# Interleaving the K and V weight transposes with their matmuls, splitting the Wd load, and sharing the softmax masks between VectorE and GpSimd

## What is computed

```python
xn = layernorm(x)
Q, K, V = heads(xn @ Wq.T + bq), heads(xn @ Wk.T + bk), heads(xn @ Wv.T + bv)   # 16 heads of 64
mask = (col <= row & row - col <= 128) | (row < 1) | (col < 1)
attn = softmax(where(mask, Q @ K.T / 8, -1e9)) @ V
a    = attn @ Wo.T + bo
w    = top-1 routing of xn @ W_router over 2 experts
r    = sum_e w[e] * ((silu(xn @ Wg[e]) * (xn @ Wu[e])) @ Wd[e])
s    = (silu(xn @ Sg) * (xn @ Su)) @ Sd
out  = x + a + r + s
```

## Time and profile before

| | |
|---|---|
| two runs | 1678.94 and 1824.74 us, median 1751.84 |
| the profiled execution | 1677.85 us |
| its span, slowest core (core 3) | 1676.1 us |
| spans of the eight cores | 1663.5 to 1676.1 us |
| PE busy / DVE / ACT / POOL, share of the span | 89% / 33% / 18% / 12% |
| mean granted TensorE clock, core 3 | 0.893 |

### The profile page before, as it was taken

The page is one execution under the profiler, slowest core; times in us unless marked ns, Lnnn a source line. Parts: engine busy times, 40 slices in busy tenths (PEclk is TensorE's granted clock), DMA queues, the critical chain, the costliest instruction groups (busy, mean ns, idle before and its releaser), DMA issues.

```text
span 1676.1 us, 26894 instructions; the slowest of 8 cores (1663.5 to 1676.1 us)
## 1 busy us (share of the span) xinstructions
PE 1487.0 (89%) x8424; PEld 721.0 (43%) x8424; DVE 555.7 (33%) x1187; ACT 301.1 (18%) x579; POOL 196.1 (12%) x258
## 2 busy tenths in 40 slices
PE   3566889769899878999999999999999999999893
PEld 2233434336666333444444444444444444444341
DVE  2432223367777421006641100066411000333332
ACT  2322220125555102330000023300000232000000
POOL 1000000000000121111111111111122111110211
PEclk9977898855555799999999999999999999999996
DMA  6220311200001253576531224764455437742776
GB/s 120 74 76 13 51 24 28 39 7 21 21 21 40 54 104 51 51 89 73 54 45 75 78 55 41 90 86 43 47 77 77 53 38 95 89 41 62 144 152 135
DMA packets 150812, 106.28 MB, mean 63 GB/s; under 512 B 105746, under 2 KB 126354, under 8 KB 150674
## 3 DMA queue, kind: packets, MB, share of 16 engines
q0 software_dynamic: 133664, 75.72, 33.9%
q1 hardware_dynamic: 7794, 16.27, 3.2%
q10 hardware_dynamic: 9216, 12.59, 3.2%
HBM read 117.60 MB, written 33.29 MB: 90 GB/s over the span
## 4 chain that ended last, share of the span: by engine, by line
PE 77%; DMA 12%; DVE 4%; issue 3%; ACT 3%; POOL 0%; DVEq 0%; POOLq 0%; SPq 0%; ACTq 0%
PE pb L827 20%; PE pb L809 20%; PE pb L881 14%; PE pb L347 7%; DMA out<-sto 6%; PE pb L640 4%; PE pb L381 3%; PE pb L600 3%; PE pb L649 2%; DMA pscr<-sto 2%; PE pb L760 1%; DMA ovl<-Wq 1%; ACT exT L618 1%; PE pbT L327 1%; DVE sto L897 1%
## 5 line engine op out<-in xcount | busy, mean ns | idle before, releaser
L881 PE MATMUL pb<-big 128*128 128x512 bf16 x1536 | 334.8, 381 | 7.3 <-DVE sto L897 7.2
L809 PE MATMUL pb<-xnT,stg 128*128 128x512 bf16 x1536 | 332.2, 379 | 0.4 <-ACT big L813 0.4
L827 PE MATMUL pb<-xnT,stg 128*128 128x512 bf16 x1536 | 332.0, 379 | 0.0
L831 DVE TENSOR_TENSOR big<-big,pb 128x512 bf16<-128x512 bf16 x192 | 132.0, 687 | 462.0 <-PE pb L827 461.9
L881 PEld LDWEIGHTS pb<-big 128*128 128x128 bf16 x1536 | 150.5, 98 | 191.1 <-issue 11.9
L813 ACT ACTIVATE big<-pb 128x512 bf16<-128x512 f32 x192 | 114.6, 597 | 657.1 <-PE pb L809 656.9
L809 PEld LDWEIGHTS pb<-xnT,stg 128*128 128x128 bf16 x1536 | 150.2, 98 | 181.8 <-issue 0.9
L827 PEld LDWEIGHTS pb<-xnT,stg 128*128 128x128 bf16 x1536 | 150.3, 98 | 181.2 <-issue 0.2
L618 ACT ACTIVATE exT<-pb 128x385 bf16<-128x385 f32 (+2 forms) x256 | 107.3, 473 | 107.9 <-PE pb L600 55.3
L347 PE MATMUL pb<-xnT,ovl 128*128 128x512 bf16 x512 | 120.3, 400 | 0.0
L902 DVE COPY sto<-pb 128x512 f32<-128x512 f32 x64 | 41.9, 687 | 178.9 <-PE pb L881 178.2
(11 more groups left out here) (136 smaller groups left out, 784.0 us busy)
## 6 DMA issues: line engine op xcount, KB each, us to landing
out<-sto POOLq DMA_DIRECT2D x96, 256.0 KB, 4.4
stg<-Wg POOLq DMA_DIRECT2D x32, 256.0 KB, 4.4
stg<-Wu POOLq DMA_DIRECT2D x32, 256.0 KB, 4.4
big<-Wd POOLq DMA_DIRECT2D x4, 2048.0 KB, 16.3
stxr<-x ACTq DMA_DIRECT2D x32, 256.0 KB, 4.7
stx<-x SPq DMA_DIRECT2D x8, 512.0 KB, 3.9
sto<-x SPq DMA_DIRECT2D x8, 512.0 KB, 3.7
pscr<-sto POOLq DMA_DIRECT2D x32, 128.0 KB, 2.6
```

Of the source, the lines that this page charges most:

```text
L809: add("tensor", (lambda f_=f_, ncs=ncs, td=td, bank=bank, sg=sg: (lambda t: t.matmul(pb[bank][:, 0:512], sg[:, 128 * td:128 * (td + 1)], x ...
L827: add("tensor", (lambda f_=f_, ncs=ncs, td=td, bank=bank, sg=sg: (lambda t: t.matmul(pb[bank][:, 0:512], sg[:, 128 * td:128 * (td + 1)], x ...
L831: add("vector", (lambda f_=f_, ncs=ncs, bank=bank: (lambda v: v.tensor_mul(big[:, H_OFF + T * f_ + 512 * ncs:H_OFF + T * f_ + 512 * (ncs + ...
L881: add("tensor", (lambda f_=f_, ntile=ntile, bk=bkv, woff=woff: (lambda t: t.matmul(pb[bk][:, 0:512], big[:, H_OFF + T * f_ + 128 * ntile:H ...
```

## The change

It has four parts. (1) The transposes of the four Wk quarters are no longer done in one piece: after each quarter come the 8 K groups that read it, by `gen_kt_itpair`. The loads move along. (2) V runs half by half: after the quarters 0 and 1 of Wv all 16 groups with ih = 0, after the quarter 3 all with ih = 1, with the quarters 2 and 3 of Wv, and then the quarters 0 and 1 of Wo, placed between runs of 8 groups. The bias DMA is started earlier. `vgen_one` itself is as before. (3) The masks of odd heads are multiplied on POOL. (4) Each down-weight buffer is loaded by four DMAs of a quarter, each with a key of its own, and a down matmul waits for its own quarter alone.

```diff
     load_w_quarter(dWk, 2, "Wk")
+    gen_kt_itpair(0)
     transpose_w_quarter(1, "WkT")
     load_w_quarter(dWk, 3, "Wk")
+    gen_kt_itpair(2)
     transpose_w_quarter(2, "WkT")
+    load_w_quarter(dWv, 0, "Wv")
+    gen_kt_itpair(4)
     transpose_w_quarter(3, "WkT")
-    load_w_quarter(dWv, 0, "Wv")
     load_w_quarter(dWv, 1, "Wv")
-    for nck in range(NC512):
-        gen_qkt_nck(KT_OFF, kt_k, 8, nck)
+    gen_kt_itpair(6)
+    add("gpsimd", lambda g: g.dma_start(out=bias_qkv[:], in_=dbv), w=["bias_qkv"], dma=True)
     transpose_w_quarter(0, "WvT")
     load_w_quarter(dWv, 2, "Wv")
     transpose_w_quarter(1, "WvT")
     load_w_quarter(dWv, 3, "Wv")
-    transpose_w_quarter(2, "WvT")
-    transpose_w_quarter(3, "WvT")
-    add("gpsimd", lambda g: g.dma_start(out=bias_qkv[:], in_=dbv), w=["bias_qkv"], dma=True)
     for ih in range(2):
...
+    for ntl in range(8):
+        vgen_one(ntl, 0)
+    transpose_w_quarter(2, "WvT")
     load_w_quarter(dWo, 0, "Wo")
+    for ntl in range(8, NT):
+        vgen_one(ntl, 0)
+    transpose_w_quarter(3, "WvT")
     load_w_quarter(dWo, 1, "Wo")
-    for ntl in range(NT):
-        vgen_one(ntl, 0)
+    for ntl in range(8):
         vgen_one(ntl, 1)
     transpose_w_quarter(0, "WoT")
     load_w_quarter(dWo, 2, "Wo")
+    for ntl in range(8, NT):
+        vgen_one(ntl, 1)
     transpose_w_quarter(1, "WoT")
     load_w_quarter(dWo, 3, "Wo")
     transpose_w_quarter(2, "WoT")
...
-                meng = "vector"
+                meng = "vector" if h % 2 == 0 else "gpsimd"
...
     def wdc_load(dWd_, dh, buf, c, tag):
-        if c != 0:
-            return
-        off = WDC_OFF if buf == 0 else WDC2_OFF
-        keys = wdc_k if buf == 0 else wdc2_k
+        off = (WDC_OFF if buf == 0 else WDC2_OFF) + 2048 * c
+        key = f"big:{off // 2048}"
...
-                        r=list(h_k(f_)) + list(wdc_k if buf == 0 else wdc2_k), w=[f"pb{bkv}"])
+                        r=list(h_k(f_)) + [f"big:{(woff + 512 * f_) // 2048}"], w=[f"pb{bkv}"])
```

More of the change, by code:

```diff
@@ L840, in gu_U @@
                         r=[f"wbc{e_idx}"] + list(h_k(f_)), w=list(h_k(f_)))
-    wdc_k = big_keys(WDC_OFF, WDC_OFF + 512 * 16)
-    wdc2_k = big_keys(WDC2_OFF, WDC2_OFF + 512 * 16)
     def wdc_load(dWd_, dh, buf, c, tag):
-        if c != 0:
-            return
-        off = WDC_OFF if buf == 0 else WDC2_OFF
-        keys = wdc_k if buf == 0 else wdc2_k
[L850 to L853, removed]
+        off = (WDC_OFF if buf == 0 else WDC2_OFF) + 2048 * c
+        key = f"big:{off // 2048}"
+        add("gpsimd", (lambda dWd_=dWd_, dh=dh, off=off, c=c: (lambda g: g.dma_start(
+            out=bass.AP(big.tensor, off, [[PSTEP_B, 128], [512, 4], [1, 512]]),
+            in_=dWd_.rearrange("(t p) d -> p t d", p=128)[:, 4 * c:4 * (c + 1), 512 * dh:512 * (dh + 1)])))(),
+            w=[key], dma=True, tag=tag)
     def d2_loads(ntile, dh):
```

## The result

The changed kernel took 1695.69 us (median of 9 runs), the kernel before 1677.27 us (median of 8 runs on the same chip). The ratio is 1.012, with a 95% interval of 1.0105 to 1.0136: slower by 18.4 us, beyond doubt but within 2%. The forecast was 1700 us, with an own range of 1689 to 1710 and a range for 8 in 10 of 1689 to 1742, worked out from an execution of 1677.85.

The account below looks back on a forecast made before the run. Bounds: a full PE in feed-forward, transposes waiting for weight quarters, attention at half clock. Bank loss 33.2 less gains 18.3 is 14.9; plus masks 6 and preloads 1, 21.9 us on 1677.85: 1700 us, own range 1689 to 1710, 8 in 10 1689 to 1742.

Parts of the forecast that it names:

- K and the way into V: Wk and Wv transposes up to V: loads hidden behind K groups, fewer waits; gains of 7.2 and 11.65 us.
- The turn-around: V groups sharing one bank: each waits for DVE's evacuation, 1.18 us at 28 boundaries, 33.2 us lost.
- V starts warm: V's matmuls: full clock from the first group, 55.3 us in place of 58.0, gain 2.7 us.
- The three quarters in the stream: Transposes between V's runs: Wv quarters 2 and 3 lose 5.05 us, one Wo quarter takes 2.05.
- the short Wo: Wo's transposes after V: still end in a wait for the last load, 14.5 us instead of 16.3, gain 1.8.
- Masks: Attention: POOL's masks of odd heads come late, 6 us lost, the middle between 1.4 and 10.4.
- The term for exclusion: Attention: DVE and POOL masks hold each other, 0.45 us late at a block's start; upper end 10.4 us in all.
- Preloads: Output projection: Wg preloads moved to the attention's end meet the first scratch transfers; 1 us lost, between 0 and 4.4.
- Wd: Down matmuls in the feed-forward part: loading the down weights in quarters costs or gains zero.
- V at half clock: Rival in V: clock falls to half, 52 us more over all V, 1752 (1726 with half of V); chance 0.13.
- POOL as the bound: Rival in the attention: excluding engines and slow POOL masks add 0.22 us per pair, 25 us, 1729; chance 0.13.
- The attention at full clock: Rival: clock held into the attention, pairs 0.31 us shorter, 34 us less, 1666; chance 0.04.

Follow-up runs that it names:

- a1_bank: The changed kernel with V's bank alternating again along the new order of groups; 1664.62 us, ratio 0.989 to the kernel before.
- a4_preload: The changed kernel with the two Wg preloads put back ahead of the attention in POOL's order, masks staying on POOL; ratio 1.0104 to the kernel before.
- the scratch edit: A key for each half row of the output projection's scratch; alone on the kernel before, ratio 0.9945.
- b3_wd: The kernel before with only the down weights loaded in quarters, a key for each; 1680.47 us, ratio 0.9991.
- b1_pin: The kernel before with V's bank held at 5 and nothing else; 1718.12 us, ratio 1.0207.

## What the prediction had right, and which of its steps failed

The forecast was 21.9 us more; measured were 18.4. The main mechanism, the lost second bank, is the one forecast. The step that failed most is the term for the masks: 6 us in the sum, 3.3 measured, 1.5 in a1_bank. Several others were off and cancelled in part, so that the closeness of the total is in part luck. By its own steps:

- **K and the way into V**, gain 7.2 + 11.65 = 18.85: measured 19.2 for the stage, 7.5 of it in K and 10.8 in the way into V. The mechanism is the predicted one, a load hidden behind 8 groups, and shown by the missing waits.
- **The turn-around**, 28 x 1.18 = 33.2: the step is right in kind and number, and 1.10 in size, 30.8 us. The 1.18 took 0.56 us from a group's last matmul to its evacuation. That is what the full-clock groups of V have before, where they follow each other without a pause. In the new stream, where a pause or transposes precede each group, it is 0.49 (last matmul of the group at 247.81 + 7 x 0.216 = 249.32, evacuation at 249.81). a1_bank has both: 0.56 in its full-clock groups that follow another, 0.49 in two that follow transposes. The copy and the 0.15 us to the next matmul were right.
- **V starts warm**, gain 2.7: partly wrong. V's first group ran at half clock, 1.8 us lost, because the clock had fallen during the Wv transposes, in the thin 6.9 us ahead of it (0.63 in 236 to 240). The three quarters in the stream cost 7.1 us, as reckoned. Behind V's last group, the stretch up to the routing takes 14.7 us instead of 19.8 (medians of the cores) with one quarter of 2.0 moved ahead of it, a gain of 3.1 where 1.8 was reckoned. Together, V to the attention came out at +32.6 instead of +33.75: the too-long turn-around and the short Wo on one side and the cold first group on the other cancelled in part.
- **Masks**, 6 between 1.4 and 10.4: mis-sized, 3.3 measured. POOL's mask is 0.92 us, not 0.88, so head 15 is 0.15 us late and not 0.10. The term for exclusion took 0.64 us in every block: 0.45 at the block's start and 0.19 at head 15. The 0.19 never came in the normal block shown, because DVE's mask of head 14 ended (406.37) just before POOL's of head 15 began (406.43). At the start the loss is 0.66 us (13.62 - 12.96), but in 3 of 14 blocks, and in a1_bank in none, since elsewhere DVE's first mask comes 0.07 us ahead of POOL's. That 0.64 and 0.66 agree is chance. The failed step is the order of arrival, read from one block of the earlier trace rows and taken for all, and then the middle between two ends, which stood for no case. The trace of the kernel before shows that this block is the exception (core 3, the start of the next block, window 460.9 to 462.4, ACT and DVE alone):

```profile
460.67 0.49 ACT L618 ACTIVATE exT<-pb 128x385 bf16<-128x385 f32 x1
461.27 1.44 DVE L630 TENSOR_TENSOR exT<-exT,mskC 128x385 bf16<-128x385 bf16 x5
462.29 0.59 ACT L731 COPY a_T<-pbT 128x512 bf16<-128x512 bf16 x1
```

  Here DVE's first mask starts 0.11 us after ACT has ended head 3 (461.16), and 1.02 us before the copy of `a_T`; so it is in eleven of the 14 full blocks. In the block of the earlier trace rows it starts 0.47 us after ACT (448.04 to 448.51), the latest of the 14. POOL takes its mask 0.14 us after ACT (406.29 to 406.43), so that it comes first in a block like that of the earlier trace rows and second in the eleven.
- **Preloads**, 1: wrong in cause. The output projection was 2.8 us longer, but a4_preload shows that it is not the preloads. The stage differs between cores (79.4 to 84.7 us before, 81.4 to 87.8 after). Most of the 2.8 us is PE's own busy time in it, 63.7 us before and 65.7 after (medians), at a granted clock of 0.92 and 0.89 (stage means); the four cores of after that take over 86 us have 0.88. Whether the low clock or the waits came first isn't shown. Over the kernels with V in halves its median is 82.7 to 87.2, over the others without the scratch edit 82.3 to 84.1. Whether the change has a part in that, through the time at which the stage starts, stays open.
- **Wd**: nothing, as said (b3_wd).
- **Rivals.** V at half clock: not so; the clock was 1.00 from the second group on with PE busy for 2.07 to 3.05 of 4 us, as the two rows of the output projection had let expect. The Trainium skill ("TensorE: Matmul & The Clock Gate", A second HAM failure mode: psum-queue depth-cycling) tells of a kernel whose clock swings because PE idles briefly between groups over its banks. V's stream here did not swing, with a pause behind nearly every group: b1_pin even rose to full clock in such a stream. POOL as the bound: not so, a pair goes on at 1.28 us (404.13 to 405.41). The attention at full clock: not so, PE still waited for Wo's last quarter:

```profile
338.14 0.70 POOL L311 DMA_DIRECT2D ovl<-Wo  x1 [22.87 <-PE pbU L327]
343.86 0.58 PE L327 MATMUL pbT<-ident_s,ovl 128*128 128x128 bf16 x4 [3.56 <-DMA ovl<-Wo]
```

  3.56 us where 4.7 was reckoned, and the clock went as before (0.50 through the attention).

## What to carry to other kernels

When the order of groups changes, look at what derives a bank or buffer from the loop indices: the expression here alternated in one order and stayed on one bank in the other. It ate the whole gain of the new order (from the end of Q to the attention 17.7 us in a1_bank, 183.0 instead of 200.7) and left that stretch 13.4 us longer than before. The price of a lost double buffer can be read before it is paid: last matmul to evacuation, the evacuation, its end to the next matmul, less one step. Before one block of a trace is taken for all, a second one is worth a look: here the one read was the exception. A key that is coarser than the transfer (one name for two halves of a row) is a wait that no data needs, and shows up as an engine that waits for its own DMA.

## What was not expected of the hardware

Two engines that hold each other up for 0.15 to 0.7 us (DVE masks of up to 1075 ns instead of 365, POOL's of up to 1076 instead of 916) cost PE nothing by it in 11 blocks of 14, and in a1_bank in all 14. And on core 1 of b1_pin the clock rose from half to full in a stream with an idle gap of 0.94 us after every 3.57 us of work.
